# Four projections ahead of a first attention and eight among its steps: an order changed in the prologue of a four-layer attention kernel

## The chip, the cores and the metric

One NeuronCore of a Trainium2 chip runs the whole program. The metric is the device time of one execution in microseconds (us). A core has a TensorE (PE, with its weight loads as PEld), a VectorE (DVE), a ScalarE (ACT), a GpSimd (POOL) and a SyncE (SP), which here only issues DMAs. Each engine works through its own list of instructions in order and waits for others by semaphores.

## What is computed

The reference is a stack of four cross-attention layers over 8 batches. The change touches only the first one, whose core is this (q, k and v of 16 heads with 64 dimensions, 256 positions):

```python
for i in range(2):                      # two chunks of 128 positions, each with its own weights
    h = einsum('od,bdl->bol', Wqkv[i], z[:, :, s:e]) + einsum('od,bdl->bol', Winj[i], u[:, :, s:e])
q, k, v = split(concat(chunks), 3, axis=1)
score = einsum('bndi,bndj->bnij', q + r_w_bias, k) / 8
prob = softmax(score)
attn_vec = einsum('bnij,bndj->bndi', prob, v)
x = norm(Wo @ attn_vec + bo + z)
```

Layer 1 (with mask and MLP), layer 2 (with mask and MLP) and layer 3 (attention with mean and standard deviation) follow on the result of each batch. All arithmetic stays the same in this case.

## The kernel before

Layer 0 of batch b+1 is worked off among layers 1 to 3 of batch b. Batch 0 has no batch ahead of it, so its layer 0 stands alone in a prologue ahead of the loop over batches. The prologue is the stretch in question.

**Projections.** q, k and v are made by twelve units: qp0 to qp3 (q of four heads each), kp0 to kp3 (k of four heads each) and vp0 to vp3 (v: vp0 and vp1 are heads 0 to 7, vp2 and vp3 heads 8 to 15, each for one half of the keys). The weights stand in W0, six pieces of 1 MB: piece 0 is q of heads 0 to 7, piece 1 q of heads 8 to 15, pieces 2 and 3 k in the same way, pieces 4 and 5 v. Each q or k unit is 16 matmuls of 128x128 (lines 574 and 576), each v unit is 4 matmuls of 128x512 (lines 581 and 582); the trace shows each fp32 matmul's records merged into rows. A unit fills one of the two PSUM banks GP and takes the other one in turn, so unit n waits until unit n-2 was copied out. q units are copied out by VectorE (line 1367), k and v units by ScalarE (lines 1128 and 1132). The list PROJ gives the order of the prologue: qp0 to qp3, kp0 to kp3, vp0 to vp3.

**Attention of layer 0** goes by four groups g of four heads and by eight steps k of two heads.
- The row maxima come first. ScalarE casts q and k of a group to bf16 (`cast`, lines 1140 and 1142, into buffers that groups g and g+2 share); TensorE makes bf16 scores in two pairs (`maxima_pair`, line 613; units (0, g, 0) and (0, g, 2)); VectorE reduces each pair (line 1393, two instructions); TensorE transposes the maxima (`shift_rows`, line 667; unit (0, g, "T")); VectorE copies them (line 1380).
- Then a step k: TensorE puts the maxima and the fp32 scores into SC (`scores0`, lines 689 and 695), ScalarE takes the exponential (line 1188), GpSimd adds halves for the denominators (line 1705), TensorE multiplies with v (`pv0`, line 712), two steps share a bank that ScalarE copies out (`evacuate`, line 1154), and TensorE sums the denominators (lines 730 and 733).
- EARLY is what stands ahead of step 0: both pairs of group 0, its T, and the first pair of group 1. The list FIRST says which other units stand in the middle and at the end of each step: T of the running group, then the next pair. `pv0` of step k-1 comes after the scores of step k.
- `mixed` runs these steps, one version of it on each engine. `mix_end` closes the layer: the quotients (lines 746 and 1441) and the output product with WO (`out_chunk`, line 759). In its midst is the unit kp0 of batch 1.

What sets the order is written out by hand in each engine's list, the same on all. In PE's, the prologue is: the twelve units, waits for constants (const_v, const_p, ld_par), EARLY, the eight steps, mix_end, the batches.

**SyncE** issues the loads in this order: z and u of batch 0 (zP, uP), W0 piece 0, the columns, pieces 1 and 2, ident, hmask and sel (work), pieces 3, 4 and 5, WO, rows, the weights of layers 1 to 3, the inputs of batch 0, and then `load_z(1)`, which waits until all q, k and v units of batch 0 were copied out (s_Q0, s_K0, s_V0 at 4) and loads z and u of batch 1 into zP and uP.

Of the kernel before, what the change touches and what calls it, by code (L numbers as in the profile page):

```python
# [68 lines left out]
EARLY = [(0, 0, 0), (0, 0, 2), (0, 0, "T"), (0, 1, 0)]  # L69
# [84 lines left out]

PROJ = [f"qp{i}" for i in range(4)] + [f"kp{i}" for i in range(4)] + [f"vp{i}" for i in range(4)]
BODY = ["wo", "kp0", "kp1", "kp2", "q1", "k1", "v1", "v1c", "qp0", "qp1", "vp0", "o1", "vp1", "oT", "m0", "m1", "k2",
        "v2", "w2", "kp3", "yT", "qp2", "q2", "vp2", "vp3", "k3", "o2", "qp3", "yT2", "v3", "n0", "n1", "w4", "q3",
        "u0", "u1"]  # L160
# [14 lines left out]
def build(nc, z_in, ctxT_in, ctx_in, mask1, mask2, mask3, w0, wo, w1qk, w1v, w1o, w1a, w1b,  # L175
          w2qkv, w2o, w2a, w2b, w3, cols_in, rows_in, ident_in, hmask_in, sel_in, out):
    with ExitStack() as stack:
# [296 lines left out]
        def _(sp):  # L474
# [3 lines left out]

            sp.dma_start(zP[:], z_in[0]).then_inc(ld_proj, 16)
            sp.dma_start(uP[:], ctx_in[0]).then_inc(ld_proj, 16)  # L480
            for i in range(6):
                sp.dma_start(W0[:, i], w0[i]).then_inc(ld_w0[i], 16)
                if i == 0:
                    sp.dma_start(cols[:], cols_in).then_inc(ld_cols, 16)
                if i == 2:
                    sp.dma_start(ident[:], ident_in).then_inc(ld_par, 16)
                    sp.dma_start(hmask[:], hmask_in).then_inc(ld_par, 16)
                    sp.dma_start(sel32, sel_in).then_inc(ld_par, 16)
# [70 lines left out]
        def _(pe):  # L559
# [244 lines left out]
            def mixed(b, steps, make):  # L804


                mix = mix_of(b)
                both = 0 <= b < B - 1

                def unit(L, g, u):  # L810
                    if u == "B":
                        spread_out(b + 1, g)
                    else:
                        make[L](g, u)

                for i in steps:
                    L, k, middle, end = mix[i]
                    if (L, k) == (3, 0):
                        for name in entry(b):
                            unit(*name)  # L820
                    if L == 0:
                        scores0(b + 1, k)
                        if k in (3, 7):
                            denominators(b + 1, k // 2 - 1)
                    else:
                        scores3(b, k)
                    for name in middle:
                        unit(*name)
                    if i:
                        before, at = mix[i - 1][:2]  # L830
                        if before == 0:
                            pv0(b + 1, at)
                        else:
                            pv3(b, at)
                        if both and (before, at) == (0, 7):
                            denominators(b + 1, 3)
                    if L == 0 and k == 4:
                        denominators(b + 1, 1)
                    for name in end:
                        unit(*name)  # L840
# [254 lines left out]
                mixed(b, range(4, 16) if more else range(8), make03)  # L1095
                mix_end(b)

            for name in PROJ:
                project(name, prologue, 0)
            pe.wait_ge(const_v, 2)  # L1100
            pe.wait_ge(const_p, 3)
            pe.wait_ge(ld_par, 48)
            make = {0: maxima0(0)}
            for _, g, u in EARLY:
                make[0](g, u)
            mixed(-1, range(8), make)
            mix_end(-1)
            every_batch(body)
# [3 lines left out]
        def _(act):  # L1112
# [21 lines left out]
            def cast(b, g):  # L1134

                k, j = (b - 1, g + 2) if g < 2 else (b, g - 2)
                if k >= 0:
                    act.wait_ge(mx_done, reduced(MX_AT[k, 0, j, 3]))
                act.wait_ge(s_K0, 4 * b + g + 1)
                act.activation(K0b[:, g % 2], K0[:, 2 * g:2 * g + 2, :], ACT.Copy)  # L1140
                act.wait_ge(s_Q0, 4 * b + g + 1)
                act.activation(Qb[:, g % 2, :], Q0[:, 2 * g:2 * g + 2, :].rearrange("p h l -> p (h l)"), ACT.Copy)\
                    .then_inc(s_Qb, 1)
# [31 lines left out]
            def mixed(b, steps):  # L1175
                mix = mix_of(b)
                for i in steps:
                    L, k, middle, end = mix[i]
                    n = SC_AT[b + (L == 0), L, 2 * k]
                    if (L, k) == (0, 4) and b >= 0 or i == 0 and L == 3:  # L1180
                        queries3(b, [(Q3, 0), (Q3, 1)])
                    if b < 0 and k == 0:
                        cast(0, 2)
                    for j in range(2):
                        act.wait_ge(sc_full, n + j + 1)
                        pr_taken(act, n + j, 1)
                        if L == 0:
                            act.activation(Pr[:, (n + j) % 4, :], SC[j], ACT.Exp, scale=0.125).then_inc(p_ready, 1)  # L1188
                        else:
                            act.activation(Pr[:, (n + j) % 4, :], SC[j], ACT.Exp, bias=bcol[:, 3 + k % 2:4 + k % 2],  # L1190
                                           scale=8.0 ** -0.5).then_inc(p_ready, 1)
                    if (L, k) == (0, 4) and b >= 0 or i == 0 and L == 3:
                        queries3(b, [(Q3b, 2), (Q3b, 3), (Q3, 2), (Q3, 3)])
                    if b < 0 and k == 1:
                        cast(0, 3)
                    if L == 0 and (k in (4, 6) or k == 2 and b < 0):
                        evacuate(b + 1, k // 2 - 1)
                    if L == 3 and k == 4:
                        sums(b, 0)
                    if L == 3 and k == 4 and b < B - 1:  # L1200
                        evacuate(b + 1, 3)
# [134 lines left out]
                mixed(b, range(4, 16) if more else range(8))  # L1336
                mix_end(b)

            for name in PROJ[4:]:
                project(name, prologue)  # L1340
            act.wait_ge(const_v, 2)
            act.wait_ge(const_p, 3)
            act.wait_ge(ld_cols, 16)
            cast(0, 0)
            cast(0, 1)
            mixed(-1, range(8))
            mix_end(-1)
            every_batch(body)
# [5 lines left out]
        def _(dve):  # L1354
# [41 lines left out]
            def mixed(b, steps):  # L1396
                mix = mix_of(b)

                def unit(L, g, u):
                    if u == "B":  # L1400
                        quotient0(b + 1, g)
                    else:
                        maxima(b + (L == 0), L, g, u)

                for i in steps:
                    L, k, middle, end = mix[i]
                    if (L, k) == (3, 0):
                        for name in entry(b):
                            unit(*name)
                    for name in middle:  # L1410
                        unit(*name)
                    if (L, k) == ((0, 5) if b < 0 else (3, 1)) and b < B - 1:
                        reciprocals0(b + 1, 0)
                    for name in end:
                        unit(*name)
# [207 lines left out]
            dve.memset(V2[:], 0.0).then_inc(const_v, 1)  # L1623
            dve.wait_ge(const_v, 1)
            dve.wait_ge(ld_cols, 16)
            for name in PROJ[:4]:
                project(name, prologue)
            dve.wait_ge(ld_par, 48)
            dve.tensor_copy(identb[:], ident[:])
# [229 lines left out]
```

## Time and profile before

| what | us |
|---|---|
| median of 3 runs (1096.37, 1096.55, 1098.66) | 1096.55 |
| profiled execution | 1094.25 |
| its span, from first to last instruction | 1092.1 |
| PE busy over the span | 955.9 (88%) |
| DVE busy | 541.6 (50%) |
| ACT busy | 484.3 (44%) |
| POOL busy | 268.1 (25%) |
| mean granted TensorE clock | 0.973 |
| prologue: first projection begins | 7.07 |
| prologue: first bf16 scores for the maxima begin | 31.80 |
| prologue: output product of layer 0 begins | 63.01 |

Times within a trace are counted from the start of the span. A busy share is an average over stretches with different limits; what the change does is read from the stretch from 7 to 63 us. In a timeline a row merges neighbouring instructions of one kind; its start is measured, the end of a matmul is modelled, so that the time a group takes in a dense stream is read from the start of one row to the start of the next (called pitch below).

### The profile page before, as it was taken

To read this page: it belongs to the slowest core of one execution; us is meant where nothing else is said; L and a number is where in the kernel's file an instruction comes from. 1 tells how busy PE (TensorE), PEld (TensorE's weight loads), DVE (VectorE), ACT (ScalarE), POOL (GpSimd) and SP (SyncE) were. 2 spreads that over 40 slices of the span, in tenths; PEclk is the share of its full clock that TensorE was granted. 3 is DMA by queue.
4 is the path that set the end of the run, shared out by engine and by line. 5 is a ranking of instruction groups with operands and counts; after the bars stand their busy time and mean duration, and the time that the engine had idled before them with its cause. 6 is when DMAs were issued, how large, how long until landed. Compare 5 with 4: busy or idle time off the path is not lost.

```text
span 1092.1 us, 21492 instructions
## 1 busy us (share of the span) xinstructions
PE 955.9 (88%) x8592; PEld 608.2 (56%) x8592; DVE 541.6 (50%) x1012; ACT 484.3 (44%) x937; POOL 268.1 (25%) x389
## 2 busy tenths in 40 slices
PE   7799999999899989999999998999899999976672
PEld 6466664666456664666547664556646665444430
DVE  2444555445645455445554555355554555443440
ACT  1424454364543545345543545445553455423233
POOL 0230220243111521223211421116112332113203
PEclk9899999999999999999999999999999999988886
DMA  9300220001310202002300113102120022002001
GB/s 372 134 2 1 78 98 27 18 5 80 106 35 1 79 18 104 25 2 82 106 19 18 37 48 107 35 2 80 50 72 24 2 83 97 27 9 77 5 2 38
DMA packets 29057, 60.14 MB, mean 55 GB/s; under 512 B 9376, under 2 KB 21024, under 8 KB 24096
## 3 DMA queue, kind: packets, MB, share of 16 engines
q1 hardware_dynamic: 28960, 58.77, 14.7%
q8 instruction: 70, 1.15, 0.4%
q14 instruction: 27, 0.22, 0.1%
HBM read 53.52 MB, written 5.24 MB: 54 GB/s over the span
## 4 chain that ended last, share of the span: by engine, by line
PE 72%; DVE 12%; issue 9%; ACT 4%; POOL 1%; DMA 1%; DVEq 0%; ACTq 0%; POOLq 0%; SPq 0%
DVE nm L1393 6%; PE PV L712 6%; PE GP L966 6%; PE GP L574 6%; PE GP L975 5%; PE GP L576 5%; PE SC L695 4%; PE GP L950 4%; PE SC L884 3%; PE GP L759 3%; PE SC L781 3%; PE GP L798 2%; PE GP L581 2%; PE PV L897 2%; PE MX L628 2%
## 5 line engine op out<-in xcount | busy, mean ns | idle before, releaser
L1393 DVE TENSOR_REDUCE nm<-MX 128x2 bf16<-128x512 f32 (+1 forms) x352 | 227.0, 689 | 169.7 <-PE MX L634 79.6
L1705 POOL TENSOR_TENSOR Psum<-Pr 128x512 f32<-128x512 f32 x56 | 71.3, 1274 | 255.7 <-ACT Pr L1188 255.7
L1190 ACT ACTIVATE Pr<-SC,bcol 128x512 f32<-128x512 f32 x128 | 81.0, 684 | 108.6 <-PE SC L781 108.6
L574 PE MATMUL GP<-zP,W 128*128 128x128 f32 x512 | 103.5, 284 | 7.1 <-DMA W<-w 7.1
L576 PE MATMUL GP<-uP,W 128*128 128x128 f32 x512 | 99.7, 277 | 0.0
L1188 ACT ACTIVATE Pr<-SC 128x512 f32<-128x512 f32 x128 | 69.6, 599 | 57.1 <-PE SC L695 57.1
L1215 ACT ACTIVATE Pr<-SC,bcol 128x512 f32<-128x512 f32 x96 | 60.8, 685 | 63.5 <-PE SC L884 63.5
L574 PEld LDWEIGHTS GP<-zP,W 128*128 128x128 f32 x512 | 78.9, 193 | 17.1 <-issue 15.3
L576 PEld LDWEIGHTS GP<-uP,W 128*128 128x128 f32 x512 | 78.5, 194 | 0.0
L1679 POOL TENSOR_TENSOR stat<-stat,half 128x1 f32<-128x1 f32 x24 | 13.6, 565 | 259.3 <-DVE stat L1560 163.1
L712 PE MATMUL PV<-Pr,V 128*64 128x256 f32 x512 | 69.4, 392 | 0.8
L695 PE MATMUL SC<-Q,K 64*128 64x256 f32 x512 | 68.6, 382 | 0.0
L975 PE MATMUL GP<-WB,work 128*128 128x256 f32 x256 | 59.3, 384 | 10.5 <-DVE work L1489 10.5
L781 PE MATMUL SC<-work,K 64*128 64x512 f32 x256 | 67.7, 598 | 0.0
L966 PE MATMUL GP<-oT,WA 128*128 128x128 f32 x512 | 63.7, 285 | 1.2 <-issue 0.8
L966 PEld LDWEIGHTS GP<-oT,WA 128*128 128x128 f32 x512 | 60.9, 199 | 5.1 <-issue 3.3
L975 PEld LDWEIGHTS GP<-WB,work 128*128 128x128 f32 x256 | 47.3, 190 | 22.3 <-issue 16.5
L884 PE MATMUL SC<-work,K 64*128 64x512 f32 x192 | 55.0, 637 | 0.0
L695 PEld LDWEIGHTS SC<-Q,K 64*128 64x128 f32 x512 | 50.9, 190 | 4.3
L1671 POOL TENSOR_TENSOR work<-qs,hmask 128x512 f32<-128x512 f32 x32 | 32.6, 1041 | 82.9 <-DVE Q12b L1467 82.9
L1128 ACT ACTIVATE K<-GP 128x512 f32<-128x512 f32 x32 | 19.1, 597 | 76.0 <-PE GP L576 76.0
L1477 DVE TENSOR_TENSOR work<-GP,cols 128x512 f32<-128x512 f32 x32 | 22.1, 691 | 61.1 <-PE GP L966 61.1
(188 smaller groups left out, 1708.4 us busy)
## 6 DMA issues: line engine op xcount, KB each, us to landing
WA<-w1a SPq DMA_DIRECT2D x8, 1024.0 KB, 4.8
WB<-w1b SPq DMA_DIRECT2D x8, 1024.0 KB, 7.3
WA<-w2a SPq DMA_DIRECT2D x8, 1024.0 KB, 5.0
WB<-w2b SPq DMA_DIRECT2D x8, 1024.0 KB, 7.1
W<-w SPq DMA_DIRECT2D x6, 1024.0 KB, 10.0
scratch<-U SPq DMA_DIRECT2D x16, 256.0 KB, 2.0
C<-scratch SPq DMA_DIRECT2D x96, 32.0 KB
zP<-z_in SPq DMA_DIRECT2D x8, 128.0 KB, 4.5
```

What stands on the lines that cost most here:

```text
L574: pe.matmul(dst, W0[:, piece, 2 * s, at:at + P], zP[:, s * P:s * P + P], start=True, stop=False)
L576: mm = pe.matmul(dst, W0[:, piece, 2 * s + 1, at:at + P], uP[:, s * P:s * P + P], start=False, stop=True)
L695: mm = pe.matmul(SC[r][:, kc * D:kc * D + D], K0[half, k, kc * P:kc * P + P], Q0[half, k, :], start=False, stop=True, skip_group_check=True)
L712: mm = pe.matmul(bank[64 * j:64 * j + 64, i * D:i * D + D], V0[:, kc, h * 64:h * 64 + 64], Pr[:, (n + j) % 4, kc * D:kc * D + D], start=(k ...
L781: pe.matmul(SC[j][:].rearrange("p (t l) -> p t l", l=D), K3[half, g % 2, kc * P:kc * P + P], Q3[half, g // 2 * 2:g // 2 * 2 + 2, :], start ...
L884: pe.matmul(SC[r][:].rearrange("p (t l) -> p t l", l=P), K[half, c, kc * P:kc * P + P], Q12[half, 4 * c:4 * c + 4, :], start=False, stop=True,
L966: mm = pe.matmul(g[:, j * P:j * P + P], WA[:, c, f * P:f * P + P], oT[:, c, :], start=(c == 0), stop=(c == 1), skip_group_check=True)
L975: mm = pe.matmul(g[:, 0:D], G[:, f * P:f * P + P], WB[:, f, :], start=(f == 0), stop=(f == 7))
L1188: act.activation(Pr[:, (n + j) % 4, :], SC[j], ACT.Exp, scale=0.125).then_inc(p_ready, 1)
L1190: act.activation(Pr[:, (n + j) % 4, :], SC[j], ACT.Exp, bias=bcol[:, 3 + k % 2:4 + k % 2], scale=8.0 ** -0.5).then_inc(p_ready, 1)
L1393: dve.tensor_reduce(dst, MX[(n + i) % 2][:].rearrange("p (a k) -> p a k", a=a), AX_X, ALU.max, negate=True).then_inc(mx_done, 1)
L1705: pool.tensor_tensor(Psum[:, c % 4, :].rearrange("p (a l) -> p a l", l=D), two[:, :, 0:D], two[:, :, D:2 * D], ALU.add)\
```

## The change

PROJ gets the order qp0, kp0, qp1, kp1, vp0, vp1, qp2, kp2, qp3, kp3, vp2, vp3, and the W0 pieces are issued in the order 0, 2, 4, 1, 3, 5 (the columns still behind piece 0; ident, hmask and sel still behind piece 2, which is now the second piece and not the third). Ahead of EARLY stand only the first four units. vp0 follows the first pair of group 0 and vp1 the second. The other six are put among the steps by START: on PE behind pv0 of the step before and ahead of the unit at the end of the step; on ACT behind the exponentials and evacuate of the step; on DVE behind the middle units. The casts of groups 2 and 3 move to steps 0 and 2, behind kp2 and kp3. PE's waits for the constants move from ahead of EARLY to ahead of the first T.

```diff
-PROJ = [f"qp{i}" for i in range(4)] + [f"kp{i}" for i in range(4)] + [f"vp{i}" for i in range(4)]
+PROJ = ["qp0", "kp0", "qp1", "kp1", "vp0", "vp1", "qp2", "kp2", "qp3", "kp3", "vp2", "vp3"]
+START = {0: ("qp2", "kp2"), 1: ("qp3",), 2: ("kp3",), 3: ("vp2",), 4: ("vp3",)}
@@ sync
-            for i in range(6):
+            for i in (0, 2, 4, 1, 3, 5):
                 sp.dma_start(W0[:, i], w0[i]).then_inc(ld_w0[i], 16)
@@ tensor, mixed, behind pv0 of the step before
+                    if b < 0:
+                        for name in START.get(k, ()):
+                            project(name, prologue, 0)
                     if L == 0 and k == 4:
                         denominators(b + 1, 1)
@@ tensor, prologue
-            for name in PROJ:
+            for name in PROJ[:4]:
                 project(name, prologue, 0)
-            pe.wait_ge(const_v, 2)
-            pe.wait_ge(const_p, 3)
-            pe.wait_ge(ld_par, 48)
             make = {0: maxima0(0)}
-            for _, g, u in EARLY:
+            for (_, g, u), name in zip(EARLY, ("vp0", "vp1", None, None)):
+                if u == "T" and g == 0:
+                    pe.wait_ge(const_v, 2)
+                    pe.wait_ge(const_p, 3)
+                    pe.wait_ge(ld_par, 48)
                 make[0](g, u)
+                if name:
+                    project(name, prologue, 0)
@@ scalar, mixed
-                    if b < 0 and k == 0:
-                        cast(0, 2)
...
-                    if b < 0 and k == 1:
-                        cast(0, 3)
                     if L == 0 and (k in (4, 6) or k == 2 and b < 0):
                         evacuate(b + 1, k // 2 - 1)
+                    if b < 0:
+                        for name in START.get(k, ()):
+                            if name[0] != "q":
+                                project(name, prologue)
+                        if k in (0, 2):
+                            cast(0, 2 + k // 2)
@@ scalar, prologue
-            for name in PROJ[4:]:
-                project(name, prologue)
+            for g in range(2):
+                project(f"kp{g}", prologue)
+                cast(0, g)
             act.wait_ge(const_v, 2)
             act.wait_ge(const_p, 3)
             act.wait_ge(ld_cols, 16)
-            cast(0, 0)
-            cast(0, 1)
+            for v in ("vp0", "vp1"):
+                project(v, prologue)
@@ vector, mixed, behind the middle units
+                    if b < 0:
+                        for name in START.get(k, ()):
+                            if name[0] == "q":
+                                project(name, prologue)
@@ vector, prologue
-            for name in PROJ[:4]:
+            for name in ("qp0", "qp1"):
                 project(name, prologue)
```

## Rows read from the trace of the kernel before

**Rows 1.** Page: span; granted TensorE clock in 40 slices, in tenths of full speed.
```profile
span 1092.1 us, 21492 instructions
...
PEclk9899999999999999999999999999999999988886
```

**Rows 2.** Windows of the prologue: length, busy (instructions) of PE, PEld, DVE, ACT, POOL, clock, DMA share, GB/s.
```profile
7.07:30.00 22.93, 22.80 (x144) 18.63 (x144) 3.50 (x6) 4.26 (x8) 0.00 (x0) 1.00 1.02 418
30.00:37.27 7.27, 1.88 (x16) 0.99 (x18) 2.88 (x5) 3.73 (x7) 0.00 (x0) 0.77 0.83 304
37.27:40.00 2.73, 2.56 (x14) 1.52 (x12) 1.36 (x3) 0.59 (x2) 0.00 (x0) 0.50 0.36 101
40.00:43.30 3.30, 3.24 (x26) 1.86 (x28) 1.52 (x3) 2.00 (x6) 1.61 (x2) 0.89 0.00 0
43.30:46.00 2.70, 2.70 (x30) 1.72 (x26) 1.31 (x3) 2.07 (x5) 1.22 (x2) 1.00 0.03 6
```

**Rows 3.** Timeline of PE, projections: start, length, engine, line, out<-in, count, [idle before].
```profile
7.07 0.77 PE L574 MATMUL GP<-zP,W 128*128 128x128 f32 x2 [7.07 <-DMA W<-w]
...
15.70 0.39 PE L574 MATMUL GP<-zP,W 128*128 128x128 f32 x2
...
22.84 1.02 PE L581 MATMUL GP<-W,zP 128*128 128x512 f32 x2
...
24.56 1.02 PE L581 MATMUL GP<-W,zP 128*128 128x512 f32 x2
```

**Rows 4.** Timeline of PE, first maxima, then steps 2 and 3 (scores, v).
```profile
31.80 0.40 PE L613 MATMUL MX<-K0b,Qb 64*128 64x256 bf16 x4 [1.92 <-ACT Qb L1142]
...
43.04 0.39 PE L613 MATMUL MX<-K0b,Qb 64*128 64x256 bf16 x4
43.27 0.38 PE L689 MATMUL SC<-nmT,sel 64*128 64x512 bf16 x2
...
44.44 1.08 PE L712 MATMUL PV<-Pr,V 128*64 128x256 f32 x8
45.45 0.39 PE L613 MATMUL MX<-K0b,Qb 64*128 64x256 bf16 x4
```

**Rows 5.** Timeline of PE, step 5, then mix_end with kp0 of batch 1.
```profile
51.65 0.39 PE L613 MATMUL MX<-K0b,Qb 64*128 64x256 bf16 x4
...
53.62 0.27 PE L667 MATMUL MX<-identb,nm 128*128 128x128 bf16 x2 [0.50 <-DVE nm L1393]
53.83 1.08 PE L712 MATMUL PV<-Pr,V 128*64 128x256 f32 x8
...
63.01 1.13 PE L759 MATMUL GP<-A0a,WO 128*128 128x256 f32 x4
...
64.84 0.38 PE L574 MATMUL GP<-zP,W 128*128 128x128 f32 x2
...
66.72 0.66 PE L746 MATMUL MX<-xb,hmask 32*64 32x256 f32 x8
```

**Rows 6.** Timelines of DVE (step 5) and ACT (kp0 and vp3 of the prologue).
```profile
52.18 1.29 DVE L1393 TENSOR_REDUCE nm<-MX 128x2 bf16<-128x512 f32 x2 [1.69 <-PE MX L613]
53.93 0.29 DVE L1380 COPY nmT<-MX 128x256 bf16<-128x256 bf16 x1 [0.46 <-PE MX L667]
...
17.68 0.60 ACT L1128 ACTIVATE K<-GP 128x512 f32<-128x512 f32 x1 [15.68 <-PE GP L576]
...
29.91 0.60 ACT L1132 ACTIVATE V<-GP 128x512 f32<-128x512 f32 x1 [1.12 <-PE GP L582]
```

**Rows 7.** Timeline of SP, then W0's second and fourth piece: count, KB, us to landing.
```profile
2.59 1.08 SPq L482 DMA_DIRECT2D W<-w  x2
...
5.34 1.54 SPq L482 DMA_DIRECT2D W<-w  x3
...
W<-w SPq DMA_DIRECT2D x1, 1024.0 KB, 7.0
...
W<-w SPq DMA_DIRECT2D x1, 1024.0 KB, 10.9
```

## Prediction

> **What bounds the kernel now.** I read the page first, then the windows over the prologue, then the timelines of PE, DVE, ACT and SP there, then the DMA issues with their landings. The span is 1092.1 us [rows 1]; the change touches the stretch up to 63.01, where the output product of batch 0 begins [rows 5]. In the windows one looks at PE's busy time against the length [rows 2]. From 7.07 to 30.00 PE is busy 22.80 of 22.93 us: twelve projections in a row, each needing nothing but weights. From 30.00 to 37.27 it is busy only 1.88 of 7.27: the first group's maxima go PE, DVE, PE, DVE, with nothing else to do on PE. The granted clock is 0.77 in that window and 0.50, which is the 1.2 GHz level, in the next (37.27 to 40.00); it is 0.89 in 40.00 to 43.30 and 1.00, the 2.4 GHz level, from 43.30. So it fell after PE had stood nearly idle and rose after it had been busy again. From 40 us on PE is full (3.24 of 3.30, 2.70 of 2.70). Two thirds of the reading lie in this: the steps of the attention are bound by PE, and only the opening of the attention is bound by a chain of waits. A projection put among the steps is therefore not free; one put into the opening is. DMA is full until about 37 us, but PE waits for it only once, at 7.07 [rows 3].
>
> **The change part by part.** First the prices. Four q or k units take 22.84 - 15.70 = 7.14, so 1.785 each [rows 3]. A v unit takes 24.56 - 22.84 = 1.72 [rows 3]. A pair of bf16 maxima has a pitch of 43.27 - 43.04 = 0.23, a step's scores (lines 689 and 695) 44.44 - 43.27 = 1.17, a step's v product 45.45 - 44.44 = 1.01 [rows 4], a T 53.83 - 53.62 = 0.21 [rows 5].
>
> A unit between groups with other array shapes costs a little more: kp0 of batch 1 takes 66.72 - 64.84 = 1.88 up to the next group [rows 5], 0.10 above 1.785. I take 0.10 for each change between full-array and 64-row shapes that the new order adds; its lower end is nothing, its upper end the 0.23 of a whole pair. The Trainium skill, TensorEngine Tiling (Array Packing), section Key Properties, says that changing the tiling mode drains the TensorE; it speaks against this change, which adds some eight such turns, and gives no figure. With no price on them the gain below would be about 0.6 us larger; with 0.10 the row agrees that there is a drain and that it is small.
>
> Chain prices: from a pair's start on PE to its reduction on DVE 52.18 - 51.65 = 0.53, two reductions 1.29, then 53.62 - 53.47 = 0.15 to the T; so 1.97 from the pair to its T [rows 5, 6]. From T to the copy 53.93 - 53.62 = 0.31, the copy 0.29 [rows 6], and I take the same 0.15 to the next matmul.
>
> Now the new order, by time. The start stays at 7.07: the first piece and z and u are issued as before. Its first matmuls run at half the later rate in either order, since nothing ahead of them changes. Four units later PE stands at 15.70, as the fifth one did before [rows 3]. Is their data there? The second piece was issued at 2.59 and landed 7.0 later, at 9.6; kp0, which now needs it, starts at 15.70 - 3 x 1.785 = 10.34 [rows 3, 7]. Margin 0.7 us, the thinnest of all. The fourth piece landed at 5.34 + 10.9 = 16.2 behind three pieces and sel; v's piece 4 now has one megabyte less ahead of it. At (16.2 - 9.6) us for two pieces and about 0.6 MB of tables, a megabyte is about 2.5 us, so it lands at 13.7 and is needed at 16.1. Pieces 1 and 3 take the places with 16.2 and about 18.7 and are needed at 22.2 and 23.9. No load stops PE, as long as the thin one holds.
>
> Is the first cast done? ACT takes a unit 17.68 - (15.70 + 1.785) = 0.20 after PE, and the first pair began 31.80 - 29.91 = 1.89 after the start of the last copy [rows 3, 4, 6]. kp0 now ends at 12.12, so its cast is ready at about 14.2, ahead of 15.80. The second cast (kp1, taken at 15.9) is ready at 17.8 and needed at 20.8.
>
> PE then: first pair of group 0 at 15.80; vp0 at 16.13 (0.23 + 0.10); second pair at 17.95 (1.72 + 0.10); vp1 at 18.28; T at 20.00 (PE is free then; DVE would allow 17.95 + 1.97 = 19.92, so both v units hide in the waits); first pair of group 1 at 20.75 (0.31 + 0.29 + 0.15); scores of step 0 at 20.98; qp2 and kp2 at 22.15; second pair of group 1 at 25.82 (3.57 + 0.10); scores of step 1 at 26.05; T at 25.82 + 1.97 = 27.79, a new wait of 0.57 that the slow clock covered before; v of step 0 at 28.00; qp3 at 29.01; pair of group 2 at 30.90 (1.785 + 0.10). Before, this last pair began at 43.04 [rows 4].
>
> From there to the output product it was 63.01 - 43.04 = 19.97 at full clock [rows 4, 5]. To this come kp3 (1.885), vp2 and vp3 (1.82 each), 5.53 in sum. The output product starts at 30.90 + 19.97 + 5.53 = 56.40 instead of 63.01: **6.6 us earlier**. All projections have their full price in this; what pays is 7.27 - 1.88 = 5.4 us of idle PE and the slow clock behind it [rows 2], less one wait and the drains.
>
> What hides the rest, edit by edit. The waits for constants on PE move behind both v units; sel now lands earlier, so they cost nothing. If sel were late, DVE's cast of it stands ahead of its first reduction and all maxima would wait. On ACT the copy of kp2 and both casts of group 2 (1.89 as above) go from 25.9 to 27.8, ahead of the exponentials of step 1, whose scores are there at 27.2. These slip 0.6 us; their v product is two steps' work off, and SC is free again before the scores of step 2. The pair at 30.90 needs the cast of 27.8. kp3 and its cast in step 2 have the same margins. On DVE, qp2 stands ahead of the reduction of the pair at 25.82 and is long there. vp3 (heads 8 to 15) must be copied before v of step 4: PE has the rest of step 4 and the scores of step 5 in between, about 2.5 us, against 0.20 + 0.60 [rows 6]. On SP, load_z(1) now waits for vp3 until about 45 instead of being issued at once; in its queue stands only the wait of batch 0's second MLP behind it, and its data is needed by kp0 of batch 1 at 64.84 - 6.6 = 58.2 [rows 5]. All other loads of batch 0 had landed by 40: the DMA share is 0.00 from there [rows 2]. So batch 0's body, which starts behind the output product, meets nothing new and moves forward as a whole, as do all batches behind it.
>
> **Against the times.** The profiled execution goes to a span of 1092.1 - 6.6 = 1085.5. It took 1094.25, which is 2.3 below the median of 1096.55. The forecast for the median is 1096.55 - 6.6 = 1089.95, say **1090.0 us**. The clock also falls below full in the last three or four slices [rows 1], where PE has gaps; the runs differ by 2.3 us among themselves, and I take 1.5 us either way for this.
>
> **The rivals.**
> *A. Forecast: the opening is filled, the rest costs its full price.* 1087.9 to 1091.5. Chance 0.68.
> *B. One more wait per step.* The new units are in order on ACT and DVE too; if an exponential or a reduction slips behind a unit that PE makes late, PE waits, as at 53.62 where it waited 0.50 [rows 5]. Five steps with 0.5 each take 2.5 us, or the thin load margin or a slow clock once more takes as much. Gain 2.5 to 5: 1091.5 to 1094.0, middle 1092.5. For it: many in-order waits. Against: each one that I followed has over 0.5 us of slack but two. Chance 0.17.
> *C. The projections hide among the steps as well.* Then the output product would come earlier by all eight units that leave the head, 15.7 by about 4 x 1.785 + 4 x 1.72 = 14 us: 1082.5. Against it: PE was busy 2.70 of 2.70 there [rows 2]. A milder form, in which the drains cost nothing, gives 7.2 to 8.6 us, down to 1087.9. Chance of a gain over 8.6: 0.05.
> *D. It does not carry through.* Something of batch 0 is bound to a time of its own, such as the late load of z for batch 1, or the last batch gives the gain back by its clock. Gain under 2.2: about 1096, range 1094.4 to 1098. Against it: no load was under way in 40.00 to 43.30 [rows 2]. Chance 0.06.
> *E. Slower.* The clock does not recover: the start runs at half rate, and if the mix of 64-row matmuls and short waits from 15.8 us on leaves TensorE at 1.2 GHz as in 37.27 to 40.00 [rows 2], each microsecond of work takes two. It decides from 6.6 us of PE work at the low level on; if the whole opening up to 30.90 ran so, with 14 us of work, the result would be 14 - 6.6 = 7.4 slower: 1104. Against it: before, the same mix kept 1.00 in 43.30 to 46.00, and the clock fell only after PE had been busy 1.88 of 7.27. Chance 0.04.
>
> **How the numbers follow.** The range holds A's and most of B's times and the small end of C's: 1087.3 to 1093.8, which leaves out D, E, strong C and the ends of B and A, some 0.2. A measurement of this kernel tells about 0.2%, 2.2 us, from no change. Faster by over 0.2% (below 1094.4): A, B and C, 0.90. Within: nearly all of D, 0.06. Slower: E, 0.04.
>
> **What would show it.** In the profile after: first pair (line 613) near 15.8, first scores (689) near 21, output product (759) near 56.4; granted clock 1.00 in all windows from 15 to 56; PE idle there under 2 us; the pitch of a unit among steps 1.8 to 1.9. The stretch from the output product to the end should be the same within 2 us. Wrong if an L574 or L581 row shows a wait for DMA, if PE waits for Qb ahead of a maxima pair, or if the clock falls.

## The result and the profile after

The changed kernel takes 1090.42 us (median of 5 runs, 1089.14 to 1092.41); the kernel before, run beside it, 1096.92 (5 runs, 1096.37 to 1098.66). The ratio is 0.9944, 95% interval 0.9927 to 0.9960: 6.5 us less, where 6.6 was forecast, and 1090.42 where 1090.0 was.

The mechanism is read best in two windows that hold the same work: all that PE does from the fifth projection, before, or from the first bf16 pair, after, up to the output product. Both hold 318 PE records. First the window of the kernel before, then the one after (columns as in [rows 2]).

```profile
15.70:63.01 47.31, 41.07 (x318) 24.54 (x317) 16.00 (x26) 20.00 (x36) 12.13 (x14) 0.93 0.46 179
```

```profile
17.72:58.98 41.26, 39.78 (x318) 23.53 (x317) 15.86 (x25) 18.37 (x33) 12.11 (x14) 1.00 0.49 187
```

The stretch is 6.05 us shorter. PE's idle time falls from 47.31 - 41.07 = 6.24 to 41.26 - 39.78 = 1.48, which is 4.76; its busy time falls by 1.29, although the work is the same. That 1.29 is a net figure: the granted clock is 1.00 instead of 0.93, and against it the new order adds turns between array shapes, about 0.1 us each, which count as busy time (see the point on the turns below).

The idle time can be followed wait by wait. Four of the six waits of the kernel before stand in these rows (the other two, 1.92 at 31.80 and 0.50 at 53.62, in [rows 4] and [rows 5]):

```profile
33.76 0.51 PE L613 MATMUL MX<-K0b,Qb 64*128 64x256 bf16 x4 [1.56 <-DVE nm L1393]
35.81 0.37 PE L667 MATMUL MX<-identb,nm 128*128 128x128 bf16 x2 [1.55 <-DVE nm L1393]
36.66 0.61 PE L613 MATMUL MX<-K0b,Qb 64*128 64x256 bf16 x4 [0.48 <-DVE nmT L1380]
...
40.06 0.95 PE L689 MATMUL SC<-nmT,sel 64*128 64x512 bf16 x2 [0.23 <-ACT Pr L1188]
```

They are 1.92 + 1.56 + 1.55 + 0.48 + 0.23 + 0.50 = 6.24 us. After, 0.48, the new 0.50 and the 0.50 of step 5 are left. So 1.92 us of the gain come from the first pair, which no longer waits for its cast, and 1.56 + 1.55 from the two waits that the v units fill; the 0.23 is gone too, and the new 0.50 goes off the sum again.

The windows of the prologue after, to be set against [rows 2]:

```profile
15.70:20.70 5.00, 5.00 (x32) 3.10 (x31) 2.93 (x6) 2.63 (x5) 0.00 (x0) 1.00 1.01 421
20.70:26.00 5.30, 4.82 (x35) 3.39 (x34) 2.67 (x5) 1.73 (x4) 0.42 (x1) 1.00 1.02 407
26.00:31.00 5.00, 4.50 (x43) 3.49 (x42) 2.28 (x4) 2.72 (x5) 0.85 (x1) 1.00 1.04 424
31.00:36.00 5.00, 5.00 (x45) 3.71 (x42) 1.89 (x3) 1.30 (x3) 1.40 (x2) 1.00 0.97 363
```

The window of 7.27 us in which PE was busy for 1.88 has no successor: PE is full but for two waits of half a microsecond, in the second and third window; the third wait, of step 5, comes at 49.59 and was there before too. The timeline of PE after shows both, and the opening itself (line numbers are larger by one: 614 is the pair, 582 and 583 a v unit, 668 the T, 690 and 696 the scores, 575 and 577 q or k units). The kernel in print shows that a row with x2 of these fp32 lines is one matmul with two records: a q or k unit is 8 matmuls with 16 records, a v unit 2 matmuls with 4 records.

```profile
8.02 0.77 PE L575 MATMUL GP<-zP,W 128*128 128x128 f32 x2 [8.02 <-DMA W<-w]
...
17.72 0.39 PE L614 MATMUL MX<-K0b,Qb 64*128 64x256 bf16 x4
18.04 1.12 PE L582 MATMUL GP<-W,zP 128*128 128x512 f32 x2
19.01 1.02 PE L583 MATMUL GP<-W,uP 128*128 128x512 f32 x2
19.96 0.39 PE L614 MATMUL MX<-K0b,Qb 64*128 64x256 bf16 x4
...
22.10 0.28 PE L668 MATMUL MX<-identb,nm 128*128 128x128 bf16 x2
22.85 0.39 PE L614 MATMUL MX<-K0b,Qb 64*128 64x256 bf16 x4 [0.48 <-DVE nmT L1390]
23.07 0.39 PE L690 MATMUL SC<-nmT,sel 64*128 64x512 bf16 x2
...
30.00 0.27 PE L668 MATMUL MX<-identb,nm 128*128 128x128 bf16 x2 [0.50 <-DVE nm L1403]
30.20 1.08 PE L713 MATMUL PV<-Pr,V 128*64 128x256 f32 x8
31.21 0.49 PE L575 MATMUL GP<-zP,W 128*128 128x128 f32 x2
31.54 0.39 PE L577 MATMUL GP<-uP,W 128*128 128x128 f32 x2
...
32.88 0.39 PE L577 MATMUL GP<-uP,W 128*128 128x128 f32 x2
33.20 0.39 PE L614 MATMUL MX<-K0b,Qb 64*128 64x256 bf16 x4
...
58.98 1.13 PE L760 MATMUL GP<-A0a,WO 128*128 128x256 f32 x4
```

Where the pair of [rows 4] had 1.92 us of idle PE ahead of it, it now follows the fourth projection at once, and vp0 and vp1 stand in the places of the next two waits (1.56 and 1.55).

Behind the output product nothing changed. A window of 880 us from there on, and what follows it to the end of the span, before and after:

```profile
63.01:943.01 880.00, 814.65 (x7454) 521.37 (x7452) 464.21 (x869) 415.73 (x809) 220.81 (x304) 1.00 0.14 48
943.01:1092.10 149.09, 91.58 (x764) 53.67 (x760) 56.21 (x109) 47.29 (x91) 34.14 (x58) 0.83 0.08 28
```

```profile
58.98:938.98 880.00, 814.65 (x7452) 521.56 (x7452) 464.19 (x869) 415.30 (x809) 220.45 (x304) 1.00 0.14 48
938.98:1088.30 149.32, 91.74 (x764) 53.80 (x760) 56.33 (x109) 47.24 (x91) 34.14 (x58) 0.83 0.08 28
```

The same PE work to 0.01 us, and the same remainder within 0.23. The prologue's gain is carried to the end one for one.

### The profile page after: what moved, and what is told of

Same layout as the page of the kernel before. It is cut to its first block, busy times and chain, and to the rows that moved or that the text cites. A ratio compares the mean times of both kernels' runs of the same rounds, so it can differ in the third digit from the quotient of the medians.

```text
span 1088.3 us, 21493 instructions
## 1 busy us (share of the span) xinstructions
PE 955.9 (88%) x8592; PEld 608.5 (56%) x8592; DVE 541.6 (50%) x1012; ACT 483.9 (44%) x937; POOL 267.7 (25%) x389
## 4 chain that ended last, share of the span: by engine, by line
PE 72%; DVE 12%; issue 9%; ACT 4%; POOL 1%; DMA 1%; DVEq 0%; POOLq 0%; SPq 0%; ACTq 0%
DVE nm L1403 6%; PE PV L713 6%; PE GP L575 6%; PE GP L970 6%; PE GP L979 5%; PE GP L577 5%; PE SC L696 4%; PE GP L954 4%; PE SC L888 3%; PE GP L760 3%; PE SC L782 3%; PE GP L799 2%; PE GP L582 2%; PE PV L901 2%; PE MX L629 2%
```

## The experiments

The theory: a projection is free only in the waits of the opening; among the steps it costs its full price; the slow clock is a part of the cost of an idle opening. The main rival was that units among the steps hide too. A second question came from the two profiles: the start. The first projection began at 7.07 us before and at 8.02 after, and ran at half rate for longer.

One table for all profiles, in us. "Pair" is the first bf16 pair of the maxima, "product" the output product. The time is the median, with its ratio to the kernel before, which was run beside it on the same chip. Rows of the table ran on different chips, unless the text says that they ran side by side.

| kernel | first projection | pair | product | pair to product | product to end | time | ratio (95%) |
|---|---|---|---|---|---|---|---|
| before | 7.07 | 31.80 | 63.01 | 31.21 | 1029.1 | 1096.92 | |
| b_again | 7.16 | 32.26 | 63.63 | 31.37 | 1029.2 | 1094.99 (1 run) | |
| changed | 8.02 | 17.72 | 58.98 | 41.26 | 1029.3 | 1090.42 | 0.9944 (0.9927 to 0.9960) |
| a_again | 7.17 | 16.29 | 57.55 | 41.26 | 1028.6 | 1088.49 | 0.9926 (0.9914 to 0.9938) |
| a_old_loads | 7.54 | 18.20 | 60.17 | 41.97 | 1029.4 | 1093.73 | 0.9969 (0.9957 to 0.9980) |
| a_dense | 8.04 | 17.83 | 58.88 | 41.05 | 1029.4 | 1090.32 | 0.9932 (0.9918 to 0.9946) |
| a_v_first | 7.12 | 20.51 | 62.91 | 42.40 | 1028.3 | 1096.11 | 0.9995 (0.9984 to 1.0006) |
| a_doubled | 7.00 | 16.05 | 67.89 | 51.84 | 1031.9 | 1102.71 | 1.0059 (1.0044 to 1.0074) |
| b_filled | 8.03 | 32.89 | 62.67 | 29.78 | 1034.4 | 1094.76 | 0.9989 (0.9977 to 1.0000) |
| a_waits | 7.04 | 15.95 | 56.08 | 40.13 | 1029.2 | 1088.69 | 0.9928 (0.9916 to 0.9940) |
| a_third | 7.43 | 16.34 | 57.60 | 41.26 | 1031.4 | 1090.90 | 0.9944 (0.9930 to 0.9957) |
| a_warm | 7.50 | 15.66 | 56.92 | 41.26 | 1028.8 | 1090.09 | 0.9935 (0.9920 to 0.9949) |
| a_waits_warm | 7.65 | 15.81 | 55.93 | 40.12 | 1030.5 | 1088.75 | 0.9923 (0.9906 to 0.9941) |
| a_halves | 5.90 | 14.40 | 55.15 | 40.75 | 1029.3 | 1088.31 | 0.9930 (0.9911 to 0.9949) |

The stretch from the pair to the product repeats to 0.01 us over the three profiles of the changed kernel; the start and the end do not. So mechanisms are judged in the middle stretch, and the whole time only says whether they arrive.

### The same kernels again

> No edit: the kernel before once more, for its prologue. Two things moved at the start between the two profiles: the first projection began at 7.07 us before and at 7.98 after, and the q and k rows ran at half rate for 2.7 us before (7 rows) and for about 4.9 us after. Theory S (it is the execution, not the order): the kernel before also shows such starts, so this profile need not repeat 7.07 and 2.7; from the end of the slow rows to the output product it shows again about 53 us, and the same 5.4 us of idle PE from 30 to 37 (plus any shift). Theory O (the new order of the loads delays the first piece): 7.07 and 2.7 again, within 0.2.

> No edit: the changed kernel once more. Theory S: the first projection somewhere from 7.0 to 8.0 us and a slow stretch of another length than 4.9; from the first bf16 pair (line 614) to the output product 41.26 us as in the first profile. Theory O: first projection at 7.98 and slow until 12.8 again. Time against the kernel before: ratio 0.994, that is 6.5 us less, by both.

> No edit: the changed kernel once more, as the measure for the two others of this call. If the difference between its executions comes from the start (first projection at 7.0 to 8.0 us, half rate for 2.7 to 4.9 us, in the profiles so far) and from the clock near the end, the stretch from the first bf16 pair to the output product is 41.26 us again. Time 1087.8 to 1091.

The first projection began at 7.07, 7.16, 7.54 (a_old_loads) and 8.03 (b_filled) with the old order of the loads, and at 8.02, 7.17 and 7.43 with the new one. Theory O falls: it is the execution, not the order. The length of the half-rate stretch differs too: from the first projection to the first pair, which is the same work each time, the changed kernel took 9.70, 9.12 and 8.91 us.

### The order of the loads

```diff
-            for i in (0, 2, 4, 1, 3, 5):
+            for i in range(6):
                 sp.dma_start(W0[:, i], w0[i]).then_inc(ld_w0[i], 16)
```

> The changed kernel with the pieces of W0 loaded in the old order 0, 1, 2, 3, 4, 5. kp0 needs the third piece (landed at 12.2 us in the profile of before) instead of the second (9.6), and vp0 the fifth (about 18.7) instead of the third. My reading: PE then waits for kp0 until about 12.2, a stop of up to 1.9 us if qp0 ends at 10.3 and nearly none if it ends at 11.7 as in the slow start; vp0 at 16.1 to 18 waits up to 2.6 us, so 1 to 4 us later than the changed kernel, with a wait for DMA in the rows of line 575 or 582. Rival (the loads' order does not matter, only the order of the units): within 0.5 us of the changed kernel. Rival O: the first projection goes back to 7.07 with the old order.

Timeline of PE:

```profile
12.68 0.46 PE L575 MATMUL GP<-zP,W 128*128 128x128 f32 x2 [1.46 <-DMA W<-w]
...
19.27 1.10 PE L582 MATMUL GP<-W,zP 128*128 128x512 f32 x2 [0.67 <-DMA W<-w]
```

PE waits for exactly the two pieces named, 2.1 us in sum. So the order of the loads is a needed part of the change: 2.1 us of it in this profile. The median is 5.2 us above that of a_again, run beside it, more than the 2.1 of the waits; the profiled execution was the fastest of its five (1091.77 us), and what the others lost beyond it was not seen.

### Units in one row ahead of the steps

```diff
 tensor, prologue
+            for name in PROJ[6:]:
+                project(name, prologue, 0)
             mixed(-1, range(8), make)
 tensor, mixed
-                    if b < 0:
-                        for name in START.get(k, ()):
-                            project(name, prologue, 0)
```

The copies and casts on ScalarE and VectorE moved with them.

> The changed kernel with the six units of START in one row ahead of the scores of step 0 instead of among the steps (same units, same banks; kp2's cast ahead of step 0, kp3's still in step 1). My theory (a unit costs its full price wherever it stands, plus a drain on entering and leaving): 5 insertions become one, so 4 x 0.2 = 0.8 us less than the changed kernel, and T of step 1 still waits 0.5; net 0.5 to 1 us less. Rival C (units among the steps hide behind waits of the other engines): this kernel is slower than the changed one by the hidden part, several us up to 10.6.

From the pair to the product 41.05 against 41.26 us. With the eight steps free of projections nothing is lost: the steps hid none of that work. The gain of 0.2 is below the 0.5 to 1 that I expected; a new wait of 0.47 took the rest:

```profile
36.00 0.87 PE L690 MATMUL SC<-nmT,sel 64*128 64x512 bf16 x2 [0.47 <-ACT Pr L1192]
```

The scores of step 1 now come right behind those of step 0 and wait for the exponentials of step 0.

### Twice the work among the steps

```diff
+            def project(name, o, k, times=1):
...
-                        for name in START.get(k, ()):
-                            project(name, prologue, 0)
+                        for name in START.get(k, ()):
+                            project(name, prologue, 0, 2)
```

> The changed kernel with the matmuls of the six units of START done twice into the same bank (the second pass overwrites the first, the result is the same). My theory (PE bound among the steps, units there cost their full price): 4 x 1.79 + 2 x 1.72 = 10.6 us later at the output product, less at most 0.5 where the second pass covers the wait for T of step 1. Rival C (units among the steps hide behind the other engines): 0 to 5 us later.

From the pair to the product 51.84 - 41.26 = 10.58 us more, where the full price was 10.6. The wait of 0.50 for the T of step 1 is still there, so the added work covered nothing. This settles rival C: a unit among the steps costs what it costs alone.

### The v units ahead of the opening

```diff
-            for name in PROJ[:4]:
+            for name in PROJ[:6]:
                 project(name, prologue, 0)
...
-            for (_, g, u), name in zip(EARLY, ("vp0", "vp1", None, None)):
+            for (_, g, u), name in zip(EARLY, (None, None, None, None)):
```

> The changed kernel with vp0 and vp1 ahead of the first bf16 pair instead of in the waits between the opening's units. My theory (only units put into the opening's waits are free): from the start of vp0 to the first scores it now takes 3.44 for the two units, 1.96 + 1.97 + 0.75 for the opening and 0.23, that is 8.4 against 5.4 in the changed kernel: 3.0 us later at the full clock. If PE's idle time in the opening also lets the clock fall, as in the kernel before, up to 2.3 us more, so 3.0 to 5.3 us later than the changed kernel at the output product. Rival (the order of the k units and of the loads brings the gain, not the filling): within 1 us of the changed kernel.

With 3.44 us of work moved out of the waits no gain is left in the time: 0.9995 (0.9984 to 1.0006). The profile keeps a small one: from the fifth unit to the output product it is 62.91 - 16.98 = 45.93 us here and 47.31 in the kernel before, as the first pair does not wait for its cast here either; these 1.4 us did not show in the median. Windows from vp0 to the first scores, and behind:

```profile
16.98:25.40 8.42, 4.80 (x24) 1.97 (x24) 2.88 (x5) 2.94 (x5) 0.00 (x0) 1.00 1.01 411
25.40:30.00 4.60, 4.60 (x30) 4.03 (x26) 1.30 (x2) 1.08 (x2) 1.27 (x1) 0.63 1.05 424
```

The first is 8.42 us, as worked out (8.4). Behind it the clock is 0.63, with PE full: it fell after PE had been idle for 3.6 of 8.42 us, and the q rows there have the pitch of the start again, 27.82 - 27.39 = 0.43 us:

```profile
27.39 0.64 PE L577 MATMUL GP<-uP,W 128*128 128x128 f32 x2
27.82 0.63 PE L575 MATMUL GP<-zP,W 128*128 128x128 f32 x2
```

In a_again vp0 starts at 16.61 and the first scores at 21.64, so that from vp0 to the output product these 45.93 us stand against 57.55 - 16.61 = 40.94: 5.0 us. Up to the first scores it is 8.42 against 21.64 - 16.61 = 5.03, so 3.4 (the full price of the two units) for the emptied waits. The remaining 1.6 lies behind the first scores, where qp2 runs at half rate; I put it down to the clock. Before the run I had set 5.4 for the 5.03.

### The clock alone

```diff
 kernel before, tensor, prologue
-            for _, g, u in EARLY:
+            for (_, g, u), fillers in zip(EARLY, (15, 11, 11, 0)):
+                for _ in range(fillers):
+                    pe.matmul(SC[0][:, 0:D], identb[:], sel[:].rearrange("p h k -> p (h k)")[:, 0:D],
+                              start=True, stop=True, skip_group_check=True)
                 make[0](g, u)
```

> The kernel before with 37 extra bf16 matmuls of 256 columns (about 0.11 us each at full clock, result thrown away) in three of the opening's waits on PE: 15 ahead of the first pair, 11 ahead of the second, 11 ahead of the T. It takes the clock apart from the idle time: the waits stay, but PE isn't idle. My theory: the granted clock stays at 1.00 from 30 to 43, and from the first pair to the pair of group 2 (31.80 to 43.04 = 11.2 us before) it takes about 9.0, so 2.2 us less than the kernel before; the other 4 to 5 us of the changed kernel's gain need the real work in the waits. Rival: the clock has no part, time unchanged within 0.5 us.

Windows of the opening:

```profile
30.00:37.00 7.00, 6.38 (x50) 4.03 (x48) 2.59 (x4) 3.04 (x7) 0.00 (x0) 1.00 0.89 328
37.00:40.00 3.00, 2.04 (x21) 1.31 (x19) 1.59 (x3) 1.80 (x4) 0.00 (x0) 1.00 0.35 95
```

The clock stays at 1.00 where it was 0.77 and 0.50 [rows 2]. From the first pair to that of group 2 it takes 42.70 - 32.89 = 9.81 us instead of 11.24: 1.4 less, not 2.2. What the slow clock had covered shows up in the timeline as a new wait of PE:

```profile
39.52 0.40 PE L613 MATMUL MX<-K0b,Qb 64*128 64x256 bf16 x4 [0.48 <-DVE nm L1396]
```

The time fell by 1.4 us (0.9989, 0.9977 to 1.0000), just at what can be told from nothing. From the first pair to the output product it is 29.78 us instead of 31.21, also 1.4 less. So the clock without the work is worth 1.4 us, about a quarter of the change's 6.05; the rest needs real work in the waits and the earlier first pair. The two parts do not simply add up, since at the full clock the chain of waits shows more idle time.

### The waits that are left

```diff
-START = {0: ("qp2", "kp2"), 1: ("qp3",), ...
+START = {0: ("kp2",), 1: ("qp3",), ...
-            for (_, g, u), name in zip(EARLY, ("vp0", "vp1", None, None)):
+            for (_, g, u), name in zip(EARLY, ("vp0", "vp1", "qp2", None)):
```

In step 1, qp3 also goes ahead of the T on PE and DVE.

> The changed kernel with qp2 right behind the first T (instead of behind the scores of step 0) and qp3 ahead of the T of step 1 (instead of behind it): two of the three waits that are left (0.48 and 0.50 us in the profile after) get real work. My theory: both waits go, 41.26 from the first pair to the output product becomes 40.3 to 40.6 (one turn between array shapes more or less is 0.1), 0.7 to 1.0 us less. Rival: the later copies on DVE (the T's copy behind qp3's) make scores wait, and nothing is gained or up to 0.5 lost.

41.26 becomes 40.13, and of the three waits only that of step 5 is left. The 1.13 us are a little more than the 0.7 to 1.0 expected. In the whole time it can't be told from the changed kernel (0.9928, 0.9916 to 0.9940, against 0.9926 and 0.9944 on other chips).

### The half rate at the start

```diff
+            pe.wait_ge(warm_v, 1)
+            for _ in range(30):
+                pe.matmul(MX[0][:, 0:D], nm0[:, 0, 0, :], nm0[:].rearrange("p g s c -> p (g s c)")[:, 0:D],
+                          start=True, stop=True, skip_group_check=True)
             for name in PROJ[:4]:
                 project(name, prologue, 0)
```

> The changed kernel with 30 bf16 matmuls of 256 columns on a zeroed tile, from about 1.2 us on, while PE waits for the first weights (result thrown away). My theory of the half rate at the start (TensorE begins at 1.2 GHz and rises once it has been busy, wherever it is in its program): the rise falls into the fillers, the q and k rows run at 0.22 us from the first one on, kp1 ends 1.3 to 2.7 us earlier against the start of qp0, and the time is 1.5 to 2.5 us less than the changed kernel. As kp0 then is due at about 9.0 and its piece lands at 9.6, PE may wait for DMA 0.5 us there. Rival (the half rate comes from the DMA traffic of the weights at the same time): rows still at 0.43 us, time unchanged.

> Both edits: qp2 and qp3 in the waits for the two T, and the fillers ahead of the first projection. If they add up: 1.1 us (41.26 to 40.13, seen) and 1.5 to 2.5 us less than the changed kernel, so 2.6 to 3.6 us less, about 1085.5 to 1086.5. Rival: the wait for kp0's piece takes back the second part, about 1087.5.

Timeline of PE in a_warm:

```profile
1.17 6.29 PE L1104 MATMUL MX<-nm 128*128 128x256 bf16 x30 [1.17 <-DVE nm L1636]
7.50 0.46 PE L575 MATMUL GP<-zP,W 128*128 128x128 f32 x2
7.79 0.39 PE L577 MATMUL GP<-uP,W 128*128 128x128 f32 x2
...
10.13 0.46 PE L575 MATMUL GP<-zP,W 128*128 128x128 f32 x2 [0.61 <-DMA W<-w]
```

Apart from the first row (7.79 - 7.50 = 0.29 us, much as the 0.30 behind the later wait for DMA) the projections run at the full pitch of 0.22 us at once, while the DMA is as busy as in the kernel before (a share of 1.02 from 7 to 10 us, 1.01 before). So the half rate does not come from the loads; it depends on what TensorE did ahead. The record of the granted clock does not show it: it says 1.00 from 7.07 to 30.00 us in the kernel before [rows 2], half-rate rows included, and only the pitch tells. As expected kp0 then overtakes its piece and waits 0.61 us. From the first projection to the pair it is 8.16 us instead of 8.91 to 9.70: 0.7 to 1.5. The time is 0.8 us below that of a_third, run beside it, and not the expected 1.5 to 2.5. In the whole time the two can't be told apart (0.9935 and 0.9944, intervals that overlap); with both edits it is 0.9923 (0.9906 to 0.9941), 1088.75 us against 1090.90 for the changed kernel beside it: 2.15 us, less than the 2.6 to 3.6 expected.

### Smaller first loads

This kernel holds both edits of a_waits_warm, with 22 fillers instead of 30, and cuts the loads that qp0 and kp0 need:

```diff
+            for i in (0, 2):
+                sp.dma_start(W0[:, i, :, 0:256], w0[i][:, :, 0:256]).then_inc(ld_half[i // 2], 16)
             for i in (0, 2, 4, 1, 3, 5):
+                if i in (0, 2):
+                    sp.dma_start(W0[:, i, :, 256:512], w0[i][:, :, 256:512]).then_inc(ld_w0[i], 16)
+                else:
+                    sp.dma_start(W0[:, i], w0[i]).then_inc(ld_w0[i], 16)
```

On PE, the units that need a first half wait for ld_half instead of ld_w0.

> The kernel with both edits (qp2 and qp3 in the waits of the T, fillers ahead of the first projection, now 22 of them) and the loads of W0's pieces 0 and 2 cut in halves of 256 columns: first the halves that qp0 and kp0 need, then the other two. My theory (the start waits for the bytes of its first two pieces at about 420 GB/s, 2.5 us a megabyte): qp0 starts 1.2 us earlier, at about 6.2 to 6.5, no wait for kp0 (0.61 us in the last two profiles), so the first bf16 pair at 13.4 to 13.9 instead of 15.7 to 15.8, and the output product near 54. Time 1.5 to 2 us less than with whole pieces, about 0.990 to 0.991 of the kernel before. Rival (rows of 1 KB instead of 2 KB make the loads slower, or PE waits for the second halves): first pair not before 15, time unchanged.

qp0 starts at 5.90, but the pair only at 14.40 and the product at 55.15 instead of 54. More than half of the expected gain stayed in other loads: the columns are now issued behind three loads (both first halves and the second half of piece 0) instead of one, DVE's copy of qp0 waits for them, and PE for that copy (0.70 us); vp0 waits 0.58 us for its piece. In PE's timeline:

```profile
10.63 0.49 PE L584 MATMUL GP<-zP,W 128*128 128x128 f32 x2 [0.70 <-DVE Q L1392]
...
15.38 1.10 PE L591 MATMUL GP<-W,zP 128*128 128x512 f32 x2 [0.58 <-DMA W<-w]
```

Its span of 1084.4 us is the shortest of all; its time, 0.9930 (0.9911 to 0.9949), is not below that of a_waits_warm and misses the 0.990 to 0.991 expected.

## Why the prediction was right, point by point

- **What bounds the prologue.** Right: shown by a_doubled (10.58 of 10.6 us) and a_dense for the steps, and by a_v_first (3.4 us for two units taken out of the waits, 8.42 where 8.4 was worked out) for the opening.
- **Idle time and clock as the two sources.** Right: 4.76 us of idle and 1.29 of busy time in the windows, the latter net of the turns. The clock was seen alone in b_filled, 1.4 us.
- **The size, and luck in it.** By the prediction the stretch of the first window should shrink from 47.31 to 40.60 us, by 6.7; it shrank by 6.05. That the median fell by 6.5, so near the 6.6, is in part luck: the two other sets of runs of the same kernels gave 8.8 (1097.29 and 1088.49) and 6.25 (1097.15 and 1090.90).
- **The steps of the opening.** From the first pair, forecast and seen: T at 4.20 and 4.38, second group's pair at 4.95 and 5.13, first scores at 5.18 and 5.35, T of step 1 at 11.99 and 12.28, pair of group 2 at 15.10 and 15.48, product at 40.60 and 41.26. Both waits in that sum came, with 0.48 and 0.50 us of idle PE: that for the copy of the first T, which I had only put into the 0.75 from T to the next pair, and the new one of step 1.
- **The turn between array shapes.** The term that was too small. Among the steps I took 0.10 us once for a unit, on leaving it. It is paid on entering too: 31.54 - 31.21 = 0.33 instead of 0.22, then 33.20 - 32.88 = 0.32. A q unit among the steps takes 33.20 - 31.21 = 1.99 us and not 1.885. In the opening I had taken it on both sides, and vp0 shows a third one: 18.04 - 17.72 = 0.32 instead of 0.23, 19.01 - 18.04 = 0.97 instead of 0.86, and 19.96 - 19.01 = 0.95 instead of 0.86. That is 0.10 too little at each of seven places (vp0, vp1, qp2 with kp2, qp3, kp3, vp2, vp3), and 41.26 exceeds 40.60 by 0.66. kp0 of batch 1 [rows 5], from which I read the price, follows the output product, which uses the full array like itself, and so shows only one of its two turns. The Trainium skill, TensorEngine Tiling (Array Packing), section Key Properties, says that a change of the tiling mode drains the TensorE; the trace agrees in so far as each turn costs about 0.10 us, and no run here shows the drain itself. The working also says that without a price on turns the gain would be about 0.6 us larger; its own steps with every 0.10 left out give 0.9.
- **The start.** I held 7.07 us and the half-rate rows of one profile for fixed. The first pair came at 17.72, 16.29 and 16.34 instead of 15.80. It did no harm to the forecast because the start varies in the kernel before just as well (7.07, 7.16 and, with fillers behind the projections, 8.03), and the gain was subtracted from a median, not from the profiled execution.
- **Loads.** The thin margin of kp0 (0.7 us) held, with the start at half rate; with the fillers, at full rate, kp0 waits 0.61 us.
- **Waits behind.** ACT, DVE and SP as forecast; load_z(1) was issued at 47.85 (about 45 was worked out), without anyone waiting for it.
- **The rest of the kernel.** Right: 880 us of equal work. The rivals B, C, D and E did not come. B's mechanism, an exponential that makes the scores wait, was seen in a_dense (0.47 us) and in the kernel before (0.23 at 40.06), not in the changed one.

What stays open: in the profiles the product begins 63.01 and 63.63 before and 58.98, 57.55 and 57.60 after, 5.3 us apart in the mean, while the medians of three sets of runs are apart by 6.5, 8.8 and 6.25. Both profiles of before (1094.25 and 1094.99) lie at the low end of its runs, so part of the difference may be that choice; it was not settled.

## What to carry to other kernels

A busy share tells where a moved piece of work is free: among steps in which the engine is full it costs its whole price, plus a turn on entering and one on leaving; in a chain of waits it costs nothing but the turns and keeps the clock up besides. So move the work that nobody needs yet behind the point where the first chain can start, and put as much of it as fits into that chain's waits; the rest only has to be out of its way. Check the order of the loads with it: with the old order two waits for weights took 2.1 us, a third of the 6.05.

## What the runs showed of the hardware

- **The start is not the same in each execution.** In the twelve profiles in which the first projection waited for the first load of 1 MB it began between 7.00 and 8.04 us. Without fillers ahead of it the first row at the full pitch came at 10.1 to 13.3 us.
- **Fillers bring the full rate before the work begins.** After 30 bf16 matmuls on zeros all projections ran at the full pitch, 0.22 us, where the first rows otherwise have 0.43. In a_waits_warm PE then even waited 1.62 us for the load, and the rate held.
- **The last stretch varies with its clock.** From the product to the end the profiles range from 1028.3 to 1034.4 us, and all of it lies behind the first 880 us: in these PE is busy for 814.4 to 814.7 us in each of the fourteen profiles. The last window of b_filled, against 149.09 us at a clock of 0.83 before:

```profile
942.67:1097.10 154.43, 97.08 (x764) 56.27 (x760) 56.34 (x109) 47.26 (x91) 33.61 (x58) 0.79 0.08 27
```

The same 764 records take 5.3 us longer, and PE's busy time is 97.08 instead of 91.58. So in this stretch, where PE has gaps, the granted clock differs between executions that do the same work (0.84 to 0.79 over all profiles). Why it does is not shown. With such differences a change of 1 us in the prologue was seen in the timelines and not in the times.
